# Moving the spread of the row degrees from TensorE to the DMA, and two pairs of heads at a time instead of one, in an attention, graph and expert layer

## What is computed

```python
adj = jnp.clip(adj + jnp.eye(n, dtype=adj.dtype), 0.0, 1.0)
deg = jnp.sum(adj, axis=-1, keepdims=True)
feats = v.reshape(b * HEADS, n, DHEAD)
for l in range(GNN_DEPTH):
    h = feats @ gnn_w[l] + gnn_b[l]
    h = jnp.einsum('bij,bjd->bid', adj, h) / deg
    feats = jax.nn.gelu(h + feats, approximate=False)
gnn_out = feats @ lin_w + lin_b
out = out + gnn_out.reshape(b, HEADS, n, DHEAD)
```

## Time and profile before

| | |
|---|---|
| time, median of 3 runs | 1184.27 us (1180.09 to 1184.78) |
| the profiled execution | 1183.16 us, of which the span of the trace is 1181.3 us |
| busy, share of the span | TensorE 92%, VectorE 77%, ScalarE 68%, GpSimd 42% |
| granted TensorE clock, mean | 0.98 of full speed, 1.00 in the loop over the batches |
| one turn of the loop over batches | 59.60 us (13 turns) |

### The profile page before, as it was taken

The page is one execution under the profiler, slowest core; times in us unless marked ns, Lnnn a source line. Parts: engine busy times, 40 slices in busy tenths (PEclk is TensorE's granted clock), DMA queues, the critical chain, the costliest instruction groups (busy, mean ns, idle before and its releaser), DMA issues.

```text
span 1181.3 us, 28227 instructions
## 1 busy us (share of the span) xinstructions
PE 1088.6 (92%) x8320; PEld 863.9 (73%) x8320; DVE 913.0 (77%) x3755; ACT 806.1 (68%) x2351; POOL 497.6 (42%) x648
## 2 busy tenths in 40 slices
PE   5999999999999999999999999999999977898993
PEld 4677777777777777777777777777777756888993
DVE  5658797979797979797979797979788895566556
ACT  4678686768686868686868686868686853565662
POOL 4324253525353534343434344444444362545444
PEclk9899999999999999999999999999999998999997
DMA  6960000000000000000000000000000011222227
GB/s 201 405 231 1 2 3 9 5 6 3 8 3 8 1 10 1 10 1 10 1 10 1 10 1 10 1 10 1 10 1 9 2 55 49 60 55 63 62 62 221
DMA packets 37311, 47.41 MB, mean 40 GB/s; under 512 B 6009, under 2 KB 28539, under 8 KB 37200
## 3 DMA queue, kind: packets, MB, share of 16 engines
q1 hardware_dynamic: 32880, 37.81, 10.2%
q0 software_dynamic: 4320, 8.47, 2.1%
HBM read 18.14 MB, written 28.58 MB: 40 GB/s over the span
## 4 chain that ended last, share of the span: by engine, by line
PE 57%; DVE 29%; issue 8%; DMA 3%; SPq 1%; POOL 1%; ACT 1%; DVEq 0%; POOLq 0%
PE bank L633 46%; DVE eb L1411 5%; DVE nmax L1396 5%; DVE ea L1408 3%; PE bank L730 3%; DVE dT L1425 2%; PE bank L1000 2%; PE bank L769 1%; PE bank L743 1%; DVE z L1445 1%; DVE ratio L1755 1%; PE bank L746 1%; PE bank L744 1%; DMA pairs<-zout,zin 1%; DVE t L1656 1%
## 5 line engine op out<-in xcount | busy, mean ns | idle before, releaser
L495 POOL TENSOR_TENSOR ea<-ea,wgt 128x256 f32<-128x256 f32 x128 | 78.3, 612 | 400.1 <-DVE wgt L1420 400.1
L1396 DVE TENSOR_REDUCE nmax<-bank 128x1 f32<-128x128 f32 (+1 forms) x512 | 152.0, 346 | 60.5 <-PE bank L633 48.4
L1086 ACT ACTIVATE gt<-bank 128x512 f32<-128x512 f32 (+1 forms) x256 | 111.5, 491 | 66.6 <-PE bank L746 66.5
L1118 ACT ACTIVATE ea<-bank,nmax 128x128 f32<-128x128 f32 x256 | 96.0, 375 | 62.3 <-DVE nmax L1396 56.5
L633 PE MATMUL bank<-gt,g 128*64 128x256 f32 (+1 forms) x1024 | 112.8, 341 | 24.3 <-DVE z L1451 24.3
L497 POOL TENSOR_TENSOR eb<-eb,wgt 128x512 f32<-128x512 f32 x128 | 132.9, 1039 | 0.0
L1118 ACT ACTIVATE eb<-bank,nmax 128x256 f32<-128x256 f32 x256 | 123.3, 482 | 0.0
L633 PE MATMUL bank<-gt,vnat 128*64 128x256 f32 (+1 forms) x1024 | 111.5, 337 | 12.0 <-ACT gvT L1086 11.0
L633 PE MATMUL bank<-qk 64*128 64x128 f32 (+1 forms) x1024 | 119.3, 351 | 0.0
L1411 DVE SCALAR_TENSOR_TENSOR eb<-idw,ssum,eb 128x256 f32<-128x256 f32 x256 | 118.4, 500 | 0.0
L633 PEld LDWEIGHTS bank<-gt,g 128*64 128x64 f32 x1024 | 65.9, 137 | 61.1 <-issue 33.6
(11 more groups left out here) (231 smaller groups left out, 3207.9 us busy)
## 6 DMA issues: line engine op xcount, KB each, us to landing
slots<-zero SPq DMA_DIRECT2D x33, 520.0 KB, 15.2
zin<-slots SPq DMA_DIRECT2D x71, 65.0 KB
got<-pairs SPq DMA_DIRECT2D x8, 512.0 KB, 6.9
raw_gu<-in_guT SPq DMA_DIRECT2D x8, 352.0 KB, 2.9
out<-x_all SPq DMA_DIRECT2D x8, 256.0 KB, 2.6
pairs<-zout,zin POOLq DMA_INDIRECT x71
dn<-in_downT SPq DMA_DIRECT2D x2, 512.0 KB, 16.6
slots<-z,row_now POOLq DMA_INDIRECT x64, 2.3
```

The costliest lines, as they stand in the source:

```text
L495: nc.gpsimd.tensor_tensor(ea[:, s], ea[:, s], wgt[:, s, 0:2].unsqueeze(2).to_broadcast([P, 2, P]), ALU.mult)
L1086: return nc.scalar.activation(o, i, ACT.Copy, **more)
L1118: done = nc.scalar.activation(e[:, s, a, :], score_bank(n, a)[:, TILE_SCORES[t]], ACT.Exp, bias=nmax[:, s, i:i + 1], accum_out=ssum[:, s, ...
L1396: done = V.tensor_reduce(nmax[:, n % 3, i:i + 1], score_bank(n, a)[:, TILE_SCORES[t]], X, ALU.max, negate=True)
```

## The change

The degrees no longer pass through GpSimd and TensorE. VectorE writes the degree of each row, one number, to a small tile `dg`; SyncE stores that of two pairs to memory, transposed, and loads it back to 64 partitions for each head of a pair (`dgb`). The load of a step stands behind the store of the next step in SyncE's list. `difference` now writes `dT`'s content to `aT`, and `attended` multiplies it there, in place, later: for pairs 0 to 3 near the end of the batch, for pairs 4 to 7 at the start of the next. `mixed_values` waits for `difference` alone. `differences`, `layer1`, `layer2_in`, `layer2`, their VectorE and ScalarE steps and the copy to `gvT` work on two pairs, 512 columns, a whole bank; the last step of layer 2 uses banks 4 and 3 for its input and output. `output_attended` of all pairs moved to the next batch. The clearing of memory at the start is cut into pieces around the first stores of degrees. All five lists were written anew in another order.

```diff
+            def degrees_out(k):
+                d_dg.wait(sp, k // DOUBLES, k % DOUBLES + 1)
+                sp.dma_start(degs[2 * k:2 * k + 2, :].rearrange("a (j p) -> p (a j)", p=P),
+                             dg[:, k % DOUBLES].rearrange("p a m t -> p (a m t)"),
+                             allow_slow_non_contiguous=True).then_inc(w_dg[k % 2], 16)
+
+            def degrees_in(k):
+                sp.wait_ge(w_dg[k % 2], 16 * (k // 2 + 1))
+                if k >= DGB:
+                    sp.wait_ge(d_a.sem, k - DGB + 1)
+                for a in range(2):
+                    sp.dma_start(dgb[a * DHEAD:(a + 1) * DHEAD, k % DGB, :],
+                                 degs[2 * k + a:2 * k + a + 1, :].to_broadcast([DHEAD, 2 * TOKENS])).then_inc(w_dgb[k % DGB].sem, 16)
...
-            def degrees(b, n):
-
-                s = n % 3
-                if n >= 3:
-                    s_deg.wait(pool, b, n - 2)
-                nc.gpsimd.tensor_tensor(deg[:, s], den[:, s, :].unsqueeze(2).to_broadcast([P, 4, DHEAD]),
-                                        rs[:, s, :].unsqueeze(2).to_broadcast([P, 4, DHEAD]),
-                                        ALU.mult).then_inc(p_deg.sem, 1)
...
-            def degrees(b, n):
-
-                p_deg.wait(pe, b, n + 1)
-                for t in range(TILES):
-                    mm = nc.tensor.transpose(
-                        bank[5][:, DEG][:, xt(t)],
-                        deg[:, n % 3, 2 * t:2 * t + 2, :].rearrange("p a c -> p (a c)"), ident[:, :])
-                mm.then_inc(s_deg.sem, 1)
+            def differences(b, d):
+
+                a_gt.wait(pe, b, 2 * d + 2)
+                if d >= 1:
+                    a_d.wait(pe, b, d)
+                for m in range(2):
+                    n = 2 * d + m
+                    mm = mixed(bank[5][:, m * TOKENS:(m + 1) * TOKENS],
+                               lambda t, a: vnat[:, t, n * P + a * DHEAD:n * P + (a + 1) * DHEAD], n)
+                mm.then_inc(s_mix.sem, 1)
...
-            def mixed_values(b, n):
-                d_a.wait(act, b, n + 1)
-                copy(gvT[:, n, :], bank[5][:, MIX]).then_inc(a_d.sem, 1)
+            def mixed_values(b, d):
+                d_d.wait(act, b, d + 1)
+                if d >= 2:
+                    s_f1.wait(act, b, d - 1)
+                copy(gvT[:, 2 * (d % 2):2 * (d % 2) + 2, :],
+                     bank[5][:, :].rearrange("p (n i) -> p n i", n=2)).then_inc(a_d.sem, 1)
...
-                V.tensor_tensor(dT[:, :], bank[5][:, MIX], vT[:, n, :], ALU.subtract).then_inc(d_d.sem, 1)
-                V.tensor_tensor(aT[:, n, :], bank[5][:, DEG], dT[:, :], ALU.mult).then_inc(d_a.sem, 1)
+            def degrees(b, d):
+                d_e.wait(dve, b, 2 * d + 2)
+                for m in range(2):
+                    s = (2 * d + m) % 3
+                    done = V.tensor_tensor(dg[:, d, :, m, :].rearrange("p a t -> p t a"),
+                                           den[:, s, :].rearrange("p (t a) -> p t a", t=TILES),
+                                           rs[:, s, :].rearrange("p (t a) -> p t a", t=TILES), ALU.mult)
+                done.then_inc(d_dg.sem, 1)
+                V.tensor_tensor(aT[:, 2 * d:2 * d + 2, :],
+                                bank[5][:, :].rearrange("p (n i) -> p n i", n=2), vT[:, 2 * d:2 * d + 2, :],
+                                ALU.subtract).then_inc(d_d.sem, 1)
+                w_dgb[d].wait(dve, b, 32)
+                V.tensor_tensor(aT[:, 2 * d:2 * d + 2, :], aT[:, 2 * d:2 * d + 2, :],
+                                dgb[:, d % DGB, :].rearrange("p (n i) -> p n i", n=2), ALU.mult).then_inc(d_a.sem, 1)
...
```

More of the change, by code:

```diff
@@ L561, in batch @@
                         scatter(routed, c)
-                degrees(b, 5)
                 graph(b, 6)
                 graph(b, 7)
-                degrees(b, 6)
-                if after is not None:
-                    deviation(after, 1, 7)
-                degrees(b, 7)
+                if before is not None:
+                    token_power(before, 0)
                 if after is None:
-                    for e in range(0, 3):
+                    for e in range(0, 4):
                         gate_up_low(e)
@@ L575, in batch @@
                     z_free.wait(pool, routed, z_free.per)
-                if after is None:
-                    for e in range(3, 6):
-                        gate_up_low(e)
                 if before is not None:
@@ L1462, in batch @@
                 maxima(b, 0, 0)
-                if routed is not None:
-                    take_logits(routed, bank[6][:, LOGITS])
-                    choose(routed, 0)
                 maxima(b, 0, 1)
-                if routed is not None:
-                    choose(routed, 1)
-                maxima(b, 1, 0)
-                adjacency(b, 0)
-                weights(b, 0)
-                maxima(b, 1, 1)
                 if before is None:
@@ L1477, in batch @@
                     norm_step(after, 0)
-                maxima(b, 2, 0)
-                maxima(b, 2, 1)
-                adjacency(b, 1)
-                adjacency(b, 2)
-                weights(b, 1)
+                if routed is not None:
+                    take_logits(routed, bank[6][:, LOGITS])
+                if before is not None:
+                    attended(before, 2)
+                if routed is not None:
+                    choose(routed, 0)
+                if before is not None:
+                    attended(before, 3)
+                maxima(b, 1, 0)
+                adjacency(b, 0)
+                maxima(b, 1, 1)
+                weights(b, 0)
                 if after is not None:
                     norm_step(after, 1)
+                if routed is not None:
+                    choose(routed, 1)
+                maxima(b, 2, 0)
+                adjacency(b, 1)
+                weights(b, 1)
+                maxima(b, 2, 1)
+                degrees(b, 0)
                 maxima(b, 3, 0)
+                maxima(b, 3, 1)
+                adjacency(b, 2)
                 weights(b, 2)
-                maxima(b, 3, 1)
+                if after is not None:
+                    norm_step(after, 2)
+                maxima(b, 4, 0)
+                maxima(b, 4, 1)
+                if after is not None:
+                    norm_step(after, 3)
+                adjacency(b, 3)
+                adjacency(b, 4)
+                weights(b, 3)
+                if after is not None:
+                    norm_step(after, 4)
+                weights(b, 4)
+                if before is None:
+                    folded_values()
+                degrees(b, 1)
                 if before is not None:
                     output_bias(before)
+                maxima(b, 5, 0)
+                maxima(b, 5, 1)
                 if routed is not None:
@@ L1494, in batch @@
                 difference(b, 0)
-                attended(b, 0)
-                adjacency(b, 3)
-                maxima(b, 4, 0)
-                weights(b, 3)
-                maxima(b, 4, 1)
-                difference(b, 1)
+                adjacency(b, 5)
+                maxima(b, 6, 0)
+                weights(b, 5)
                 if routed is not None:
                     take_places(routed, bank[7][:, PLACES])
-                attended(b, 1)
+                if after is not None:
+                    norm_step(after, 5)
+                degrees(b, 2)
+                maxima(b, 6, 1)
                 if routed is not None:
```

563 lines of the change are left out of this document (258 added, 305 removed).

## The result

| | before | after |
|---|---|---|
| median, measured side by side | 1183.71 us (1180.09 to 1185.17, 6 runs) | 1190.66 us (1188.72 to 1193.22, 6 runs) |
| ratio, 95% interval | | 1.0066 (1.0045 to 1.0087) |
| span of the profiled execution | 1181.3 us | 1189.0 us |

A forecast was written before the change was run, and what follows sets the result against it. The loop was taken as bound by TensorE's own work, with VectorE close behind. From the profiled 1183.2 us, -5 (13 turns), -3 (batches 0 and 1) and +3 (end) gave 1178, forecast as 1179 us; range 1154 to 1206.

The forecast's parts named there:

- the saving on TensorE: Loop: removing eight pairs' transposes saves 1.8 us of TensorE work a turn, leaving 55.3 of 57.09 us busy.
- the edges: Outside the 13 turns: batches 0 and 1 give -3 us, batch 15 and what follows +3 (-3 to +8).
- the rival of late degrees: Turn start: store and load over 20 us together make VectorE wait before `attended`; 1207 to 1310 us, chance 0.04.
- the quiet turn: Loop: a turn was forecast as 32.1 + 10.9 + 15.4 + 0.8 = 59.2 us, against 59.6 before.
- P: Time into a turn when VectorE finishes `place_tokens`, which pair 5's graph awaits: 32.1 us, range 30 to 34.
- then pair 6's transposes, layer 1 and layer 2's input, 2.4: TensorE chain after `place_tokens`: 2.4 us from pair 6's transposes to pair 7's, which come at P + 10.9.
- what can be held up: VectorE steps with both inputs in SBUF beside GpSimd: each costs between nothing and 1.7 us, one `graph`.
- The +1.0 for the eight small products: VectorE: eight small degree products at 0.1 to 0.16 us each add 1.0 us a turn.
- 13 turns at -0.4: -5: Loop term of the sum: 13 turns, each 59.2 instead of 59.6 us, save 5 us.
- 8 us are hidden by the work between: DMAs: degree store and load, about 4 us each, are covered by 20 to 30 us of other work.
- TensorE keeps pace: Rival: few VectorE steps held up, P 30 or less, turn about 57.4 us; 1154 us, chance 0.31.
- Slower: Rival: `place_tokens` comes at 34 us or later, turn 61.1 us or more; 1204 us, chance 0.26.

The follow-up runs named there:

- experiment 9: Changed kernel with pairs 6 and 7's degree products behind the second layer1_out and degree stores in 16-byte pieces: 1156.23 us, ratio 0.9771 to the kernel before.
- Experiment 1: Changed kernel without stores and loads of the degrees, `dgb` filled once with rows of x: 1188.86 us, ratio 1.0054 to the kernel before.
- 10: Changed kernel without degree transfers and with pairs 6 and 7's degree products behind the second layer1_out: 1151.40 us, ratio 0.9734 to the kernel before.
- 4: Kernel before with unused stores of 1024 single numbers and loads added, six expert weight loads behind them: 1224.22 us, ratio 1.0361.
- 11: Kernel before with the same unused stores and loads added, but stores in 16-byte pieces: 1187.32 us, ratio 1.0046.
- experiment 2: Changed kernel with the single-number stores but without the loads, `dgb` filled once from x: 1199.76 us, ratio 1.0149 to the kernel before.
- 5: Changed kernel with pairs 6 and 7's degree products moved behind the second layer1_out on VectorE: 1178.69 us, ratio 0.9971 to the kernel before.
- 6: Changed kernel with GpSimd's four scatters behind pair 7's graph instead of pair 5's: 1210.48 us, ratio 1.0248 to the kernel before.
- experiment 12: Changed kernel with later degree products, 16-byte stores and GpSimd's wait for place_tokens behind pair 5's graph: 1160.93 us, ratio 0.9808 to the kernel before.

## Why the prediction was right and wrong

**Right: the saving on TensorE and the edges.** A turn's busy time fell from 57.09 to 54.3 us where 55.3 was forecast, so the saving was larger than the 1.8 us of the transposes; what the other 1.0 is made of I didn't trace. Batches 0 and 1 gave 2.7 (forecast 3), the end cost 4.0 (forecast 3, range to 8). Store and load of the degrees land in 2.1 (experiment 9's store; for the changed kernel's the trace gives no landing) and 2.9 us, and no `attended` waits for them: the rival of late degrees is out.

**Right by two errors: the quiet turn.** Forecast 59.2, measured 59.2. In it `place_tokens` was done 30.2 us into the turn, not 32.1: the next batch's normalising, for instance, which I had allowed the 2.19 us of the earlier trace rows, took 0.6. Pair 6's transposes came at P + 8.6 (forecast 8.5). But pair 7's came at P + 13.1 instead of P + 10.9. The 2.2 us were lost at the step "then pair 6's transposes, layer 1 and layer 2's input, 2.4": between them TensorE stood 1.5 us for `layer1_out`. The term that was mis-sized is the one on what can be held up. I priced such a step at no more than 1.7 us, "the length of one `graph`", and although I named the small products among those that can be hit, the chain behind P has nothing for them. It was 3.27 us, the length of two graphs back to back, and it stood on the path. In experiment 9, where nobody waits for it, pair 7's transposes come 2.4 us behind pair 6's, as that step has it:

```profile
522.78 0.33 PE L755 MATMUL bank<-ident,ea 128*128 128x128 f32 x1 [1.00 <-POOL eb L525]
525.25 0.27 PE L755 MATMUL bank<-ident,ea 128*128 128x128 f32 x1
```

The Trainium skill ("SBUF — State Buffer", "Who interferes with whom") says that such a VectorE instruction and a GpSimd instruction that reads SBUF exclude each other for a whole instruction. The trace agrees in kind and goes further: one product was held through four GpSimd instructions, which followed each other without a gap. The +1.0 for the eight small products was their own time, not their price.

**Wrong: "13 turns at -0.4: -5".** The sum took one turn's length for all. Two costs were missing from it.

- *The clock.* I counted a pause as its own length. Experiment 1, which has no transfers, shows what the order alone costs: 59.84 a turn, where its quiet turns take 59.15; the 0.7 us between them, 9 us in 13 turns, is the clock at 1.2 GHz behind the pauses. With the pause of 1.4 us removed (10), the clock stays at 1.00 in all turns and a turn is 57.13. So that one held step costs 2.7 us a turn, 37.5 us in all (1188.86 to 1151.40): 1.4 as the pause, 0.7 as the clock, and 0.6 beside the pause. These 0.6 show where two quiet turns are laid side by side, of experiment 1 (from 497.86) and 10 (from 480.30):

```profile
539.01 1.10 PE L638 MATMUL bank<-gvT,gw 128*128 128x256 f32 x4 [1.40 <-DVE z L1442]
540.25 1.13 PE L638 MATMUL bank<-gw,f1T 128*128 128x128 f32 x8
```

```profile
519.88 1.03 PE L638 MATMUL bank<-gvT,gw 128*128 128x256 f32 x4
520.75 1.05 PE L638 MATMUL bank<-gw,f1T 128*128 128x128 f32 x8
```

Layer 1 begins 1.6 us later in the turn (41.15 against 39.58), layer 2's input 1.9 (42.39 against 40.44). The last transpose ahead of the pause takes its whole 0.27 us of room instead of 0.11, and layer 2's input waits 0.14 more, for ScalarE's copy to `g`, which stands behind the same `layer1_out`.

- *The stores.* "8 us are hidden by the work between" was true of the data and not of the side effect. Between experiment 1 and the changed kernel they cost 0.2 us a turn, 3 in the loop.

Together: 13 x (59.15 - 59.6) = -5.8, +9 for the clock, +2.7 for the stores, +6 measured. The +9 and the +2.7 are differences between kernels; in the changed kernel itself the two mix, since two of its six falls of the clock come behind late counts (experiment 1 has seven falls and no late count).

The two causes hide each other. With both there, 1190.7; without the stores 1188.9, with the products later 1178.7; without both 1151.4, or 1156.2 in the form that computes all. So the transfers cost 2 us in the changed order, which is within the noise, and 27 in the better one. In the kernel before, single numbers cost 37 us more than pieces of 16 bytes (4 against 11), 27 of them in the loop. That a late count does no harm while TensorE stands anyway is argued, and experiment 2, the same order with 11 us lost to its stores, speaks against it; what is shown is the times.

**The rivals.** "TensorE keeps pace", 1154 us at 57.4 a turn, is what experiment 9 became, 1156 at 57.6. Its condition, P near 30, was met in the changed kernel already (30.2 in both), so P alone did not decide it; the held step behind P did. "Slower" came, but by another way than the one named for it: P of 34 never came. What I wrote would upset the forecast, a hidden wait in the first 30 us, did not; it was behind them.

## What to carry to other kernels

Before a small VectorE instruction with both inputs in SBUF is put into the list, look at what GpSimd does then: here its price was the rest of GpSimd's unbroken run, 3.27 us, and it was paid by what stood behind it, so put it where nothing urgent follows. A DMA that is hidden in time can still cost if it consists of many single numbers; keep a few numbers together and undo the order in the reader, which has a price of its own (1092 ns instead of 687 here). A mean over turns is not a turn: read the quiet turn and the long one apart, because one wrong step in a sum can be covered by another, and two causes can each look harmless alone.

## What the runs showed of the hardware

- While stores of 1024 single numbers were in use, TensorE's semaphore counts reached VectorE and ScalarE late and held them for up to 5.1 us (the longest "remote" wait, experiment 2, behind the loop), while TensorE itself went on. It happened in all kernels that had these stores (2, 4, 5, 6 and the changed one) and in none without. Loads of 2 KB rows did not do it, nor did stores in pieces of 16 bytes. There is a pattern in time: before each of the 13 late counts of experiment 2 the packets of a store had begun, 7.5 to 11.5 us earlier and mostly 9 to 10, although these packets were through in 0.7 us. The Trainium skill ("DMA: Bandwidth & Descriptors", "Rules for kernel authors") warns of one descriptor per element for a strided last dimension; the packet counts above agree, and what it doesn't say is this effect on another engine. What holds the counts stays open, also whether the recording of so many packets has a part in it: all executions shown were timed in the same way.
- The same pauses let the clock fall in one turn and not in the next (experiment 1: 59.15 and 60.4 in turn). A fall cost 1.3 us in a turn there and 2.1 in experiment 12. The pauses just ahead of the six falls in the changed kernel were 1.4 to 2.2 us long.
- A VectorE product of four numbers per row with both inputs in SBUF took 0.15 us beside an idle GpSimd and 3.27 us beside four GpSimd instructions without a gap between them, in all 13 turns of experiment 1.
